# Starting a GpSimd indirect DMA at another point of a recurrent step

## The reference

```python
xW = jnp.einsum('ntd,dh->nth', x, Wx) + b
next_h = jnp.tanh(xw_t + prev_h @ Wh)                  # for each of 1024 steps
logits = x_flat @ gate_w.T                             # x_flat: all next_h
top_v, top_i = jax.lax.top_k(logits, 2)
probs = jax.nn.softmax(top_v)
hidden = jax.nn.silu(x_flat @ wge.T) * (x_flat @ wue.T)   # for each of 8 experts
acc = acc + we[:, None] * (hidden @ wde.T)
x = x + acc
```

## Time and profile before

| | before |
|---|---|
| median of 3 runs | 873.41 us (873.13 to 873.74) |
| the profiled execution | 872.37 us |
| its span, first to last instruction | 870.6 us |
| mean granted TensorE clock | 0.897 |
| busy: TensorE, VectorE, ScalarE, GpSimd | 748.4, 443.4, 479.5, 138.9 us |
| indirect DMAs: scatters, wide additions, narrow half additions | 64, 30, 20 |

### The profile page before, as it was taken

One profiled execution on the slowest core, in us unless ns is written; L12 is line 12 of the kernel. 1 busy time (PEld: TensorE's weight loads), 2 busy tenths in 40 slices (PEclk: granted clock), 3 DMA queues, 4 the chain that ended last, 5 costly groups with the idle time before them and its releaser, 6 DMA issues.

```text
span 870.6 us, 41966 instructions
## 1 busy us (share of the span) xinstructions
PE 748.4 (86%) x17106; PEld 650.6 (75%) x17106; DVE 443.4 (51%) x2572; ACT 479.5 (55%) x2839; POOL 138.9 (16%) x134
## 2 busy tenths in 40 slices
PE   6555555799999999999989999999999999998794
PEld 4444444688888888888888888888888888888794
DVE  4776767353544445454544445454545445455452
ACT  4777778354555556454545556455545555554342
POOL 1010001002011211102120111211021112123232
PEclk7555555599999999999999999999999999997998
DMA  4776767301111111111120111111111111111211
GB/s 130 196 209 190 197 187 192 123 22 28 21 31 19 34 22 27 28 21 32 19 39 16 30 22 27 31 25 25 18 37 19 31 22 29 23 19 28 34 28 23
DMA packets 35631, 49.02 MB, mean 56 GB/s; under 512 B 5713, under 2 KB 22097, under 8 KB 35409
## 3 DMA queue, kind: packets, MB, share of 16 engines
q1 hardware_dynamic: 27200, 36.53, 15.4%
q0 software_dynamic: 7968, 9.58, 7.6%
q10 hardware_dynamic: 272, 0.26, 0.1%
HBM read 35.57 MB, written 12.88 MB: 56 GB/s over the span
## 4 chain that ended last, share of the span: by engine, by line
PE 78%; DVE 8%; ACT 7%; issue 4%; DMA 2%; another core or an unknown queue 0%; POOLq 0%; SPq 0%; ACTq 0%; DVEq 0%
PE bank L474 36%; PE bank L597 23%; PE bank L619 12%; DVE state L1174 5%; ACT bank L843 5%; PE bank L628 3%; PE bank L456 1%; PE bank L576 1%; DMA arena<-w_all 1%; PE bank L568 1%; ACT w_hi L829 1%; DVE w_lo L1149 1%; DMA b_sb<-bias_in 0%; DVE arena L1102 0%
## 5 line engine op out<-in xcount | busy, mean ns | idle before, releaser
L1174 DVE TENSOR_TENSOR state<-bank,state 128x4 f16<-128x4 f32 x1024 | 166.1, 162 | 375.9 <-ACT bank L843 355.4
L474 PE MATMUL bank<-state,wh_hi 128*128 128x4 f16 (+1 forms) x4204 | 265.2, 168 | 103.9 <-DVE state L1174 98.6
L843 ACT ACTIVATE bank<-bank 128x4 f32<-128x4 f32 x1024 | 161.9, 158 | 332.3 <-PE bank L474 322.5
L474 PEld LDWEIGHTS bank<-state,wh_hi 128*128 128x128 f16 x4204 | 177.1, 99 | 194.0 <-DVE state L1174 140.6
L474 PE MATMUL bank<-state,wh_lo 128*128 128x2 f16 x4096 | 245.4, 163 | 0.0
L474 PEld LDWEIGHTS bank<-state,wh_lo 128*128 128x128 f16 x4096 | 177.6, 97 | 0.0
L835 ACT ACTIVATE state<-bank 128x4 f16<-128x4 f32 x1024 | 175.0, 171 | 2.8 <-PE bank L474 2.7
L597 PE MATMUL bank<-x_T,w_hi 128*128 128x128 f16 (+1 forms) x1856 | 155.4, 207 | 3.6 <-issue 2.1
L619 PE MATMUL bank<-arena,w_hi 128*128 128x128 f16 (+1 forms) x1600 | 141.6, 209 | 0.0
L597 PE MATMUL bank<-x_T,w_lo 128*128 128x128 f16 (+1 forms) x928 | 138.7, 207 | 0.0
L597 PE MATMUL bank<-arena,w_hi 128*128 128x128 f16 (+1 forms) x1344 | 131.5, 213 | 2.4 <-issue 2.2
(11 more groups left out here) (141 smaller groups left out, 1025.0 us busy)
## 6 DMA issues: line engine op xcount, KB each, us to landing
arena<-w_all SPq DMA_DIRECT2D x96, 256.0 KB
xrow<-expert_rows SPq DMA_DIRECT2D x82, 66.0 KB
early<-xT SPq DMA_DIRECT2D x17, 128.0 KB
expert_rows<-pad SPq DMA_DIRECT2D x8, 132.0 KB
expert_rows<-rows,slot POOLq DMA_INDIRECT x64
out<-y_sb,place_wide POOLq DMA_INDIRECT x30
out<-y_sb,place_now POOLq DMA_INDIRECT x20, 3.1
arena<-wh_in ACTq DMA_DIRECT2D x1, 256.0 KB, 4.3
```

Source lines behind the costliest of these rows:

```text
L474: return pe.matmul(out, w[:, k, m * P:(m + 1) * P], moving, start=False, stop=False, skip_group_check=True)
L843: act.activation(h32_at(n), preact(n), ACT.Tanh, scale=1 / SCALE).then_inc(s_h32, 1)
L1174: v.tensor_tensor(lo[:, i, :, B * tt:B * tt + B], h32_at(n).rearrange("p (c b) -> p c b", c=2), hi[:, i, :, B * tt:B * tt + B], ALU.subtra ...
```

## The change

Three edits, all for GpSimd's indirect DMAs.

- The scatters' places are 0, 6 and 12 instead of 0, 3, 6 and 9. As the count hangs on the fourth scatter, it moves too.
- A scatter waits for the end of a piece of ScalarE work in the step before its own, by `pin_to`: the cast of the hidden values where that step has one (places 5, 11, 17 and 23), the halving copy of the weights in the early steps, else the tanh as before.
- The waits of the additions are written in another order, the one for the weighing (`s_y`) first, except in the loop of the tail.

```diff
-ADD_AT, SCATTER_AT = (16, 22), (0, 3, 6, 9)
+ADD_AT, SCATTER_AT = (16, 22), (0, 6, 12)
...
+            def pin_to(n):
+
+                p, o = pair_of(n)
+                half, w = divmod(o, HALF_T)
+                chunk = split_of(n // STEPS, n % STEPS)
+                if p >= 0 and w in HI_AT:
+                    pool.wait_ge(s_hhi, 2 * (2 * p + half) + HI_AT.index(w) + 1)
+                elif chunk is not None:
+                    pool.wait_ge(s_ch, chunk + 1)
+                else:
+                    pool.wait_ge(s_h32, n - FIRST)
+
             def scatter_rows(blk, n, at=None):
 
                 half, k = divmod(n, 2)
                 if at is not None:
-                    pool.wait_ge(s_h32, at - FIRST - 1)
+                    pin_to(at - 1)
                 pool.wait_ge(s_rt, RT * blk)
...
             def add_half(p, half, weighed, added, s=s_scat):
 
-                pool.wait_ge(s_acc, 32)
-                pool.wait_ge(s_y, weighed)
+                if fixed(weighed):
+                    pool.wait_ge(s_y, weighed)
+                    pool.wait_ge(s_acc, 32)
+                else:
+                    pool.wait_ge(s_acc, 32)
+                    pool.wait_ge(s_y, weighed)
                 pool.wait_ge(s_scat, added)
...
                 elif half == 0:
+                    pool.wait_ge(s_y, parts(p) + 1)
                     pool.wait_ge(s_acc, 32)
-                    pool.wait_ge(s_y, parts(p) + 1)
                     pool.wait_ge(s_scat, 16 * parts(p))
```

## The result

| | before | changed |
|---|---|---|
| median | 873.27 us (872.78 to 873.74, 4 runs) | 895.62 us (895.02 to 898.47, 4 runs) |
| ratio | | 1.026 (95% interval 1.024 to 1.029) |
| profiled execution, its span | 872.37, 870.6 us | 895.48, 893.7 us |
| mean granted TensorE clock | 0.897 | 0.900 |

Slower by 22.3 us, where +4.1 was forecast: the right direction and inside the stated range, but far off in size.

The account below looks back on a forecast made before the run. The prediction took the recurrent step chain, mostly TensorE's products, as the bound, with GpSimd's indirect DMAs lengthening steps. Additions -13.2, scatters -13.0 and tail +30.3 gave +4.1 on 873.41: 877.5 us, own range 871.5 to 885, stretched to 908.

Parts of the forecast that it names:

- The tail: After the recurrence: later counts leave over 64 rows for some experts, so seven loop pairs instead of four, +30.3 us.
- The 13 slices: Work list: 13 of the slices 0 to 34 see one block fewer, as counts are ready up to 15 steps later.
- The starting points: GpSimd's DMAs: additions begin 0.17 into step 16 instead of 0.66, scatters 0.10 into the next step instead of 0.43.
- The mechanism: Some way into an indirect DMA, no tanh gets products until about +1.33 to +1.45 us; first handoff due inside waits.
- Rival 3: GpSimd's DMAs: cost belongs to the DMA wherever it begins; no saving, tail still longer, 903.7 us; chance 0.06.
- take it as let through: Scatters' first handoff, due at +0.60, passes and the second costs 0.17 us: 48 scatters save 13.0 us.
- rival 1: Scatters' first handoff is caught at +0.60, costing 0.80 us each instead of 0.17: 907.7 us; chance 0.17.
- mixtures: Combinations of the first three rivals (scatters caught, additions caught, starting point irrelevant); chance 0.06.
- rival 2: Additions' first handoff is caught at +0.53, 30 x 0.60 us more: 895.5 us; chance 0.05.
- The additions' term: 30 wide additions and first halves of 3 narrow pairs each cost 0.20 us, saving 0.40: -13.2 us in all.
- The sum: Whole kernel: additions -13.2, scatters -13.0 and tail +30.3 give +4.1 us.

Follow-up runs that it names:

- Run 2: The kernel before with only the scatters' places changed to 0, 6 and 12, still started by the tanh: 903.8 us, ratio 1.036.
- run 15: The changed kernel, with the scatter at place 12 waiting for a one-column ScalarE copy behind the cast, so starting about 0.1 us later: 892.3 us, ratio 1.020.
- run 7: The changed kernel with the scatters' third place at 18 instead of 12: ratio 1.018.
- Run 1: The kernel before with only the additions' waits reordered, `s_y` first: 868.9 us against 874.6, ratio 0.993.
- run 3: The kernel before, old places and counts, scatters started by `pin_to`: 0 and 6 behind the cast, 3 and 9 behind the silu: 876.7 us, ratio 1.003.
- run 8: The changed kernel with scatter places 0, 3, 6 and 9, those of 3 and 9 behind a tanh: 888.5 us, ratio 1.012.
- run 9: The changed kernel with scatter places 0, 5, 6 and 11 and the count five steps ahead of the fourth scatter: 880.6 us, ratio 1.004.
- run 13: The changed kernel with scatter places 0, 4, 6 and 10 and the count four steps ahead of the fourth: 864.1 us against 874.3, ratio 0.989.
- run 14: The changed kernel with SyncE's load of the next pair's rows waiting for the tanh of step 13: 909.2 us, ratio 1.036.

## Why the prediction was right in kind and wrong in size

- **The tail: right.** 26 halves, seven loop pairs, +30.9 for +30.3. Run 2 shows that the places alone do it. (The four scatters spread over 24 steps instead of 9 in ten of the fifteen blocks; in five it was 21 before. The 13 slices are right.)
- **The starting points: right.** 0.10 into the step for scatters, 0.18 for additions (forecast 0.17).
- **The mechanism: right.** A DMA costs the end of the held stretch less the due time of the first handoff in it. By start in the step, where the first handoff passes: 0.10 cost 0.18; 0.18 cost 0.25; 0.20 cost 0.28 (run 15); 0.36 to 0.47 cost 0.40 (run 7); 0.43 cost 0.44 and 0.66 cost 0.60 (before). Rival 3 is out: runs 1 and 15 gain by starting points alone.
- **The step that failed: "take it as let through", at the scatters.** 16 of the 48 in the steps were caught, so the term was -2.3 us instead of -13.0. I had put the scatters' edge later than the additions' because an addition's handoff at +0.55 was 0.08 late and a scatter's at +0.44 not at all. But those are two different due times, and say nothing of whose edge is later. And I reckoned all 48 as one case. The runs put the edge at my very +0.60 and let it move: at places 0 and 6 handoffs due at +0.594 to +0.599 passed, while at place 12, in narrow pairs, and 2.2 us behind another scatter, those due at +0.595 were caught. The outcome is a mixture of rival 1 and the forecast; I gave mixtures 0.06.
- **Luck.** That 895.6 is also rival 2's 895.5 means nothing: 26 of the 30 wide additions passed. It lies inside the stated range only because that was stretched to reach rival 1; the forecast's own range, 871.5 to 885, misses it.
- **The additions' term was mis-sized:** -7.0 instead of -12.0 for the 30 wide ones; those at a block's start and in narrow pairs were caught (0.83 to 0.86 by the first handoff), and the first halves of the first two narrow pairs cost 0.14 and 0.15 more each where I had 0.4 gained. Run 1 gives -5.8 for the whole edit.
- **The sum** -7.0 + 0.3 - 2.3 + 30.9 = +21.9, against 23.1 between the two spans; most of the rest lies in the last steps, where the lengthened steps of several DMAs overlap and can't be put down to one.
- The Trainium skill, "SBUF — State Buffer", section "Who interferes with whom", says that "PE and ACT never wait on anyone". That section is on ports. TensorE's matmuls do start in time (264.99), as the sentence has it, but ScalarE stood 0.94 us idle, waiting for TensorE, before the tanh at 266.03: what came late is the handoff between the two. The prediction calls L1109 a cast; it is a subtraction, which changes nothing there.

**Open:** what opens the held stretch earlier at place 12. The amount of TensorE's work, its second wait, the length of ScalarE's copy and SyncE's load are ruled out, one by one. That there is a copy at all, ScalarE's wait for it, and VectorE's work there were not tried. In block starts and narrow pairs TensorE has more and shorter matmuls ahead of the products; whether that matters there was not tried either. A scatter in a narrow pair was caught even when due at +0.50 (0.89, run 15). And what in the DMA holds TensorE's handoff back, no run shows.

## What to carry to other kernels

Where a latency-bound chain crosses a GpSimd indirect DMA, count its handoffs in the DMA's own time and place the start so that one slips through with 0.1 us to spare: run 15 started 0.1 us later, and each scatter cost 0.28 instead of 0.73. Keep such starts 2.9 us apart, and look what else lands near them. And when a table of places moves, redo every count that hangs on it: here a rounding to 64 rows outweighed all savings.

## What the runs showed of the hardware that I had not expected

- Spacing decides. 1.23 us between two scatters' starts hold the handoff back for one long stretch (2.26 us between two tanhs); at 2.2 us the second scatter's handoff at +0.60 is caught; at 2.8 us and more it passes (runs 3, 8, 9, 13).
- Behind such a stall, 1.56 us long, the granted clock was 0.72 on average in the next 4 us (run 8), and 0.871 over the whole run where before it is 0.897.
- An ordinary load by SyncE near an addition raised its price from 0.37 to 0.66 us on average (run 14).
- The edge is clear-cut: handoffs due at +0.594 to +0.599 at places 0 and 6 and let through came at most 0.06 us late, yet caught ones come some 0.7 us late. When the stretch opens differs from step to step: by +0.50 in a narrow pair (run 15), not before +0.599 at places 0 and 6.
